# The output bias as a three-row product on PE, and the residual's product with the second gate on DVE, in a fused attention and expert layer

## The reference

```python
h = layernorm(x) * (1 + ca) + sa
x = x + ga * (attention(h) @ w_out + b_out)          # ga: the first gate, a row of 256 for each batch
h = layernorm(x) * (1 + cb) + sb
x = x + gb * experts(h)                              # gb: the second gate
```

## Time and profile before

| what | us |
|---|---|
| median of 3 timed runs | 1009.81 |
| span of the profiled execution | 1005.9 |
| PE busy in it | 722.7 (72%) |
| POOL busy | 653.6 (65%) |
| DVE busy | 543.6 (54%) |
| ACT busy | 376.4 (37%) |
| first stage, to the last exp | about 608 |
| from there to the first load of experts' rows | about 100 (608 to 708.3) |
| second stage | about 298 (708.3 to 1005.9) |

### The profile page before, as it was taken

The page is one execution under the profiler, slowest core; times in us unless marked ns, Lnnn a source line. Parts: engine busy times, 40 slices in busy tenths (PEclk is TensorE's granted clock), DMA queues, the critical chain, the costliest instruction groups (busy, mean ns, idle before and its releaser), DMA issues.

```text
span 1005.9 us, 15544 instructions
## 1 busy us (share of the span) xinstructions
PE 722.7 (72%) x4732; PEld 472.7 (47%) x4732; DVE 543.6 (54%) x1990; ACT 376.4 (37%) x827; POOL 653.6 (65%) x624
## 2 busy tenths in 40 slices
PE   4689998996987987987978774200699898888200
PEld 2345554553553553554554443200588776777100
DVE  3566588877877778786777673520122222222028
ACT  2145654553553553553533431100254333333100
POOL 5115340885885886885885556777388888888630
PEclk9789998996996997997996978555799999999655
DMA  8695976447446536524524558400699998898978
GB/s 301 182 345 171 357 252 222 138 158 229 160 144 228 171 127 207 180 102 156 165 94 143 169 155 253 132 8 4 202 257 283 259 251 160 154 164 173 227 210 327
DMA packets 165133, 191.58 MB, mean 190 GB/s; under 512 B 21497, under 2 KB 146581, under 8 KB 165052
## 3 DMA queue, kind: packets, MB, share of 16 engines
q1 hardware_dynamic: 128636, 134.27, 41.7%
q0 software_dynamic: 30720, 38.03, 18.6%
q10 hardware_dynamic: 5696, 18.30, 4.9%
HBM read 100.77 MB, written 110.67 MB: 210 GB/s over the span
## 4 chain that ended last, share of the span: by engine, by line
PE 32%; issue 18%; DVE 15%; DMA 14%; POOL 10%; SPq 4%; ACT 3%; another core or an unknown queue 3%; POOLq 0%; ACTq 0%; DVEq 0%
DMA acc_d<-ys,xg 8%; POOL acc_d L729 6%; PE stageA L957 4%; PE scores L985 4%; PE outT L1027 4%; DVE junk L1254 4%; PE scoresT L1007 3%; PE scoresT L1186 3%; SPq L355 3%; PE scoresT L1011 3%; DMA xt<-L_attn_x_dram 2%; PE stageA L967 2%; PE stageC L1064 2%; DVE pairs L1319 2%
## 5 line engine op out<-in xcount | busy, mean ns | idle before, releaser
L645 POOL DMA_INDIRECT slots_d<-H,dest x256 | 258.4, 1010 | 108.7 <-issue 62.7
L729 POOL DMA_INDIRECT acc_d<-ys,xg x128 | 198.2, 1548 | 61.0 <-issue 29.3
L1254 DVE CUSTOM_DVE_ANT_0 junk<-scores,mask 128x256 bf16<-128x256 f32 x512 | 187.9, 420 | 90.2 <-PE scores L985 63.7
L783 ACT ACTIVATE PT<-scoresT 128x512 f32<-128x512 f32 (+1 forms) x320 | 154.7, 508 | 151.5 <-PE scoresT L1011 104.4
L1186 PE MATMUL scoresT<-xgT,wgu 128*128 128x256 f32 x512 | 127.7, 393 | 23.6 <-ACT xgT L878 22.8
L985 PE MATMUL scores<-Ks,Qs 96*128 96x256 bf16 x512 | 108.8, 298 | 45.9 <-DVE mrowmax L1254 33.8
L1007 PE MATMUL scoresT<-mask,identb 128*128 128x512 bf16 (+1 forms) x320 | 117.6, 368 | 20.7 <-ACT PT L783 7.2
L1186 PEld LDWEIGHTS scoresT<-xgT,wgu 128*128 128x128 f32 x512 | 96.3, 194 | 48.4 <-ACT xgT L878 32.8
L1011 PE MATMUL scoresT<-Qs,Ks 98*128 98x256 bf16 (+1 forms) x640 | 118.1, 268 | 0.0
L1027 PE MATMUL outT<-PT,Va 128*32 128x256 f32 (+1 forms) x1280 | 95.0, 371 | 0.0
L598 POOL TENSOR_TENSOR r<-p,parts 128x512 f32<-128x512 f32 x32 | 39.2, 1224 | 77.8 <-ACT parts L775 76.3
(11 more groups left out here) (195 smaller groups left out, 1222.0 us busy)
## 6 DMA issues: line engine op xcount, KB each, us to landing
xg<-slots_d SPq DMA_DIRECT2D x64, 324.0 KB
slots_d<-blank ACTq DMA_DIRECT2D x26, 648.0 KB, 5.3
parts_d<-parts SPq DMA_DIRECT2D x32, 384.0 KB
Qs<-parts_d SPq DMA_DIRECT2D x96, 128.0 KB
Ks<-parts_d SPq DMA_DIRECT2D x90, 128.0 KB
acc_d<-zero SPq DMA_DIRECT2D x32, 272.0 KB
wgu<-L_ffn_w_gate_dram SPq DMA_DIRECT2D x64, 128.0 KB, 2.8
wgu<-L_ffn_w_up_dram SPq DMA_DIRECT2D x64, 128.0 KB, 2.9
```

The costliest lines, as they stand in the source:

```text
L645: pool.indirect_dma_start(out=slots_d[:, :], in_=H2[bt.par][:, t, :], in_offset=None, out_offset=bass.IndirectOffsetOnAxis(ap=dest[bt.par] ...
L729: pool.indirect_dma_start(out=acc_d[ACC[e]][:, :], in_=ys[e % NY][:, h, :], in_offset=None, out_offset=bass.IndirectOffsetOnAxis(ap=xg[e % ...
L783: sc_.activation(PT[m % NPT][:, :, 0:w], src, ACT.Exp).then_inc(sems["exp"], 1)
L1254: ins = v.tensor_tensor_reduce(out=junk[:, i, :], in0=bS[n % 2][:, i * 2 * P:(i + 1) * 2 * P], in1=mask[:, edge, :], scale=1.0, scalar=TAK ...
```

## The change

The bias goes to PE. Once, in the pass of batch 0 (slots 6 and 7), DVE splits b_out into three bf16 rows whose sum is b_out to 32 bits, and puts row 0 of the first part, row 1 of the second and row 2 of the third into one tile bo3, twice side by side (8 instructions, `out_bias`). In each `c_op` a bf16 product of three rows of ones with bo3, 512 columns wide, opens the bank, and the products with w_out are added to it. `c_xb` and its wait go; `c_x1` waits for the loads of xc and mr instead. `c_xs` moves from POOL to DVE, one slot earlier (10 for 11), and the store of x1 in SP's order one slot later (11 for 10). Behind the loop, `c_xs(last)` stands at the end of DVE's work for the last batch. The splits stay on POOL.

```diff
-    xb=(2,), onT=(2, 3), op=(4, 5), x1=(4, 5), x1_store=(10,), xs=(11,), ...
+    onT=(2, 3), op=(4, 5), x1=(4, 5), x1_store=(11,), xs=(10,), ...
 # POOL
-            def c_xb(bt):
-                after(pool, "c_ld", bt, 32)
-                after(pool, "xb", bt, 0)
-                gp.tensor_tensor(gbo[:], mr[:, 0, :], bo[:], ALU.mult).then_inc(sems["xb"], 1)
-                after(pool, "xb", bt, 1)
-                gp.tensor_tensor(xc[:], xc[:], gbo[:, :].unsqueeze(1).to_broadcast([P, T, D]), ALU.add
-                                 ).then_inc(sems["xb"], 1)
-            def c_xs(bt):
-                after(pool, "xn2", bt, T)
-                gp.tensor_tensor(x1[:], x1[:], mr[:, 3, :].unsqueeze(1).to_broadcast([P, T, D]), ALU.mult
-                                 ).then_inc(sems["xs"], 1)
...
             last = batch(B - 1)
             pre = batch(B - 2)
-            c_xb(last)
             for i in range(10):
                 send(pre, i)
             for half in range(2):
                 c_rstd(last, half)
-            c_xs(last)
 # PE, c_op
+                if bt.b == 0 and n == 0:
+                    pe.wait_ge(s_bo, 8)
+                mm(bank[:, :], onesb[0:3, :], bo3[0:3, :, :].rearrange("p i d -> p (i d)"), start=True, stop=False,
+                   skip_group_check=True)
...
-                                  start=(k == 0), stop=(k == C - 1))
+                                  start=False, stop=(k == C - 1), skip_group_check=True)
 # DVE
-                after(dve, "xb", bt, 2)
+                after(dve, "c_ld", bt, 32)
...
+            def c_xs(bt):
+                after(dve, "xn2", bt, T)
+                v.tensor_tensor(x1[:], x1[:], mr[:, 3, :].unsqueeze(1).to_broadcast([P, T, D]), ALU.mult
+                                ).then_inc(sems["xs"], 1)
+            def out_bias(part):
+                if part == 0:
+                    dve.wait_ge(s_par, 16 * 5)
+                    v.tensor_copy(selb[:], bo[:]).then_inc(s_bo, 1)
...
+                    for _ in at("xs", slot) if prev else []:
+                        c_xs(prev)
...
             e_key(last, LATE["cnt"])
+            c_xs(last)
```

More of the change, by code:

```diff
@@ L64 @@
     exp=10 * QUADS, pv=10 * QUADS, oTs=QUADS, oTp=QUADS, rec=QUADS, on=QUADS,
-    onTp=C, onT=C, op=2, t1=2, xb=2, x1=2, xs=1, stats2=T, aggr2=T, rstd2=8, xn2=T, h2=4, h2Tp=C, h2T=C,
+    onTp=C, onT=C, op=2, t1=2, x1=2, xs=1, stats2=T, aggr2=T, rstd2=8, xn2=T, h2=4, h2Tp=C, h2T=C,
     lg=1, ex=1, route=38, pre=T + 1, idc=1, cntp=1, key=2, near=T,
@@ L76 @@
     split=(-1, 0, 0, 1, 1, 2, 8, 8, 9, 9, 10, 10), store=(1, 3, 10, 11), stack=(4, 12), v=(9, 11, 13),
-    xb=(2,), onT=(2, 3), op=(4, 5), x1=(4, 5), x1_store=(10,), xs=(11,), stats2=(4, 5), c_rstd=(5, 6), xhat=(6, 7), norm2=(7, 8),
+    onT=(2, 3), op=(4, 5), x1=(4, 5), x1_store=(11,), xs=(10,), stats2=(4, 5), c_rstd=(5, 6), xhat=(6, 7), norm2=(7, 8),
     h2T=(9, 10), lg=(11,), route=(12, 13, 13, 14, 14, 15, 15, 16, 16, 17, 18, 18), cnt=(18,), key=(19,), zero=(3,),
@@ L191, in build @@
         s_fg = sem("gate_rows_loaded")
+        s_bo = sem("out_bias_steps")
         def sbt(stack, name, shape, dt=F32):
@@ L261, in build @@
         mr = sb("mr", [P, 4, D])
-        gbo = sb("gbo", [P, D])
+        bo3 = sb("bo3", [P, 2, D], BF16)
         x1 = sb("x1", [P, T, D])
@@ L663, in body @@
                         a_rstd(bt)
-                    for _ in at("xb", slot) if prev else []:
-                        c_xb(prev)
                     for half in at("c_rstd", slot) if prev else []:
@@ L671, in body @@
                         a_split(bt, n)
-                    for _ in at("xs", slot) if prev else []:
-                        c_xs(prev)
                     if now.b >= 2:
@@ L1310, in c_norm @@
                                     (ALU.mult, ALU.add)[k]).then_inc(sems["h2"], 1)
+            def c_xs(bt):
[6 more added lines that the diff above has]
+                    v.tensor_copy(selb[:], bo[:]).then_inc(s_bo, 1)
+                    dve.wait_ge(s_bo, 1)
+                    v.tensor_tensor(ex[:], bo[:], selb[:], ALU.subtract).then_inc(s_bo, 1)
+                    dve.wait_ge(s_bo, 2)
+                    v.tensor_copy(bo3[:, 1, :], ex[:]).then_inc(s_bo, 1)
+                    dve.wait_ge(s_bo, 3)
+                    v.tensor_tensor(sc[:], ex[:], bo3[:, 1, :], ALU.subtract).then_inc(s_bo, 1)
+                else:
+                    v.tensor_scalar(bo3[:, 0, :], selb[:], ident[:, 0:1], None, ALU.mult).then_inc(s_bo, 1)
+                    dve.wait_ge(s_bo, 5)
+                    v.scalar_tensor_tensor(bo3[:, 0, :], bo3[:, 1, :], ident[:, 1:2], bo3[:, 0, :], ALU.mult, ALU.add
+                                           ).then_inc(s_bo, 1)
+                    dve.wait_ge(s_bo, 6)
+                    v.scalar_tensor_tensor(bo3[:, 0, :], sc[:], ident[:, 2:3], bo3[:, 0, :], ALU.mult, ALU.add
+                                           ).then_inc(s_bo, 1)
+                    dve.wait_ge(s_bo, 7)
+                    v.tensor_copy(bo3[:, 1, :], bo3[:, 0, :]).then_inc(s_bo, 1)
             def c_route(bt, part):
@@ L1443, in body @@
                         mod_gates(slot - 1)
+                    if not prev and 6 <= slot <= 7:
+                        out_bias(slot - 6)
                     if u == 2 and ahead[0]:
```

## The result

The changed kernel took 998.11 us (median of four runs, 991.67 to 1004.87), the kernel before 1010.25 beside it (median of four, 1009.03 to 1015.16). The ratio is 0.9871, 95% interval 0.9826 to 0.9915. Forecast was 976; the time lies in the range of 960 to 1000. The profiled execution took 1000.8 us with a span of 999.1, so 6.8 us of span are to be explained, of 34.1 forecast. It is one execution, 2.7 us above the median. It also shows that start and end take 1.7 us outside the span, not the 3.9 assumed ahead of the prediction; that moves the forecast by 2 us and changes nothing else.

The account below looks back on a forecast made before the run. Passes are paced by short waits between PE, ACT and DVE; POOL alone sets the second stage's start. Terms -10.6-12.2-8-2.3-6+3.5+1+0.5 = -34.1 take the span from 1005.9 to 971.8, time 976 us (own range 966 to 986).

Parts of the forecast that it names:

- what slots 14 to 17 hold: Slots 14 to 17, batches 2 to 6: 106.0 us, 35.0 above batch 1, laid to held DVE steps, clock, sends, loads.
- the tail, -10.6: Behind the loop: POOL's sends no longer wait for the residual's sum and product, so the next send starts 10.6 us earlier.
- DVE held by POOL's product, -12.2: Slots 12 and 13: five long DVE steps held beside POOL's product return to normal, 12.2 us, all on the chain.
- what follows, -8: Slots 14 to 17: a third of the remaining 22.8 us (low clock, POOL's late sends, loads) comes back, 8 us.
- rival 2: Slots 14 to 17 fall to batch 1's length everywhere: -49, 961 us; chance 0.15.
- rival 1: Slots 14 to 17 stay long; only the tail, direct holds and slot 2 pay: -20, 990 us; chance 0.20.
- Slot 2, -2.3: Slot 2: without POOL's gbo step, DVE's second M step is no longer held, 0.47 us in five passes.
- transfers earlier, -6: Stores and loads from slot 2 come 3.1 us earlier, easing slot 8's M rows transfer: 1 us in six passes.
- PE's bias, +3.5: PE in the loop: 14 bias products of 0.22 to 0.43 us ahead of c_op's products add 3.5 us.
- DVE's product, +1: End of slot 10: DVE's product, 1225 ns in seven passes, mostly hidden, adds 1 us (0 to +16.8).
- Rival 4: Slower: DVE's product delays slot 11's maxima, PE's clock falls, bias costs 6: +24.5, 1034 us; chance 0.06.
- The steps that split the bias, +0.5, at most 2.5: Batch 0: the 8 small DVE steps, some 2.5 us in two slots, add 0.5 us, at most 2.5.

Follow-up runs that it names:

- the second chip: Changed kernel and kernel before rerun unchanged, on the second group's chip (979.3 us before): changed kernel 954.06 us, ratio 0.9741.
- the chip of the third group: Changed kernel rerun unchanged beside the kernel before, on a chip at 1009.6 us before: 1002.84 us, ratio 0.9929.
- the small product: Kernel before, with POOL's product of the residual with the second gate cut to 8 of 256 columns: 999.75 us, ratio 0.9904.
- seven sends first: Changed kernel with later bias rows; behind the loop seven sends, first half's norm steps, one send, second half's, instead of ten sends ahead: 993.42 us, 0.9834.

## Why the prediction was wrong

**The step that failed first: what slots 14 to 17 hold.** The prediction took the excess of slots 14 to 17 over batch 1, 35.0 us, as the price of VectorE's held steps, their clock and POOL's backlog, and gave 12.2 and 8 of it back. On the second chip, with product and sends where they were, the kernel before shows 84.7 us, and the change takes 5.3. The held steps were real there too (3.00, 3.16, 3.17, 2.80 and 1.63 us beside a product of 2.36) and the change removed them. Slot 15 of the five passes became 11.3 us shorter by it, but slots 14 and 17 grew by 2.8 and 3.3; what held them then has not been traced. The rest of the excess goes with the late updates: of unexplained waits the first profile had 126.8 us in ACT and DVE and the second 0.8. That sum overstates them, since all waits of the two engines between the first send and the load of rows are 376.5 us against 313.2, 63 more. The cue was in the page I read: waits "<-remote" on a single core, and long waits of ACT and DVE "<-issue".

**The step that cost most: the tail, -10.6.** On the first chip it came out at +1.6, and at +3.6 on the chip of the third group against the first chip's profile (98.1 to 99.7 and to 101.6). What failed there is "DVE did not wait for POOL's sum there but for PE, so this moment does not come earlier", read as if it would not come later either: the last step of the statistics starts 16.4 us behind the last exponential in the kernel before, and 26.5 and 26.4 in the two profiles of the changed one. Where updates come at once the tail gained 14.2, and the measured 88.1 us lies next to the 87.5 forecast. That is right as a mechanism, for POOL's sends then set the end alone, but the size is in part luck: there DVE did wait for POOL's sum, 10.29 us, and POOL 7.80 us for the gate rows instead of 3.01, and it is one profile of each kernel.

**Why later?** Six profiles are from chips with late updates. In the two whose POOL stands idle while the last inputs, gate rows and weights are loaded (the kernel before and its version with the small product), ACT's copy of the last outputs starts 3.4 and 1.3 us behind the last exponential, and the second copy of turned outputs at 7.5 and 5.9. In the four whose POOL sends all the time, 5.4, 8.3, 5.9 and 8.2, and 16.7, 16.5, 17.3 and 14.6. So the sends, which the change lets run at once, seem to be what makes updates late there, and to undo their own gain. The rest of the first stage speaks for it too: in all six profiles ACT and DVE together have at most 0.2 us of unexplained waits ahead of the first send (180 to 189 us), though 36 of the 96 loads of stacked queries are issued by then, and the first of PE's updates over 0.5 us late comes at 200 to 210 us. Against it: the second stage has another 128 indirect transfers from POOL and no update that late. These kernels differ in more than the sends, and the edits meant to isolate them met chips without the effect: it is likely, not shown.

**DVE held by POOL's product, -12.2, and what follows, -8.** Together 5.3 in slots 14 to 17 on the second chip and 8 on the first. Batches 2 to 6 gained 13.8 and 11.0 us in all; on the second chip the rest is in slots 4, 10, 11 and 19. On the second chip the stretch is nearly batch 1's (15.9 against 14.1 a pass), as rival 2 had it, but 21 of the 35 us it meant to win had never been the kernel's. On the first chip it stayed long, as rival 1 had it, and the tail's loss made it less than rival 1's 20 us.

**Slot 2, -2.3, and transfers earlier, -6.** Slot 2 itself did not move. Over five batches slot 4, where the attention output's first half is taken up, lost 3.4 us on the second chip and 1.7 on the first, slots 9 to 11 together 2.8 and 1.0, none of it forecast there; slot 8, where I expected the transfers to pay, did not move: 5.4 us before and after.

**PE's bias, +3.5.** Slots 5 and 6 grew by 1.5 and 1.6 us over five batches and slot 7 gave 1.6 back. The bias product has a mean of 384 ns:

```profile
L1043 PE MATMUL stageC<-bo,onesb 3*128 3x512 bf16 x14 | 5.4, 384 | 0.0
```

**DVE's product, +1.** Not contradicted: nothing measurable. It takes 1.2 to 1.8 us on the first chip, and on the second 2.8 in four of eight cases. The split that meets it takes 1.94 instead of 1.17. By the rule of the Trainium skill quoted in the prediction ("SBUF — State Buffer", "SBUF: two separate sides") each can hold the other, and these rows agree. Rival 4 needed this on the path and found it hidden.

**The steps that split the bias, +0.5, at most 2.5.** Wrong by some 3 us. Batch 0 takes 66.0, 63.8 and 63.3 us in the three profiles of the changed kernel, 60.8 to 66.1 in the nine other kernels with these steps in slots 6 and 7, 60.1 to 61.2 in the four with them in slots 15 and 16, where the eight take 2.91 us, and 58.0 to 59.7 in the four without them. Slot 9 shows the price without the scatter of the start: 6.9 to 8.7 us in the twelve profiles with them in slots 6 and 7, 4.2 in the eight others. I had counted their length and not that splits would hold two of them, or that the M step stands behind them. With the steps in slots 15 and 16, slot 19 is 0.8 us longer; what is left lies in slots 1 to 5, which take 16.1 to 20.8 us whatever the kernel.

In sum, for the two profiles of the first chip: +11.3 in the tail (to the load of rows, -10.6 against +0.7), +9.1 in the batches and +7.1 in batch 0 make 27.5 of the 27.3 us that the span missed.

## What to carry to other kernels

A wait that ends at nothing the profile shows need not be a property of the kernel: here the same programs had 127 us of them on one chip and 1 on another. Sum such waits before a stage's excess over another is laid to the change, and measure on a second chip. Moving work off an engine pays what that engine was last for, and a held step counts only as far as someone waits for its result. Put one-time set-up steps where nobody waits, and price them with what can hold them.

The lowest medians are those of the change with the bias rows built in slots 15 and 16: 952.1 and 952.0 us, 0.971 and 0.9723, where the change alone has 0.9741 (the intervals overlap). On the other kind these rows were tried only together with seven sends first: 0.9834, where the change alone has 0.9929.

## What the runs showed of the hardware

Semaphore updates can be recorded microseconds behind the instruction that makes them, on some chips and not on others, for the same program: 979 to 981 us on four chips, 1010 on two. Every chip was met in one session only, so the chip cannot be told from its circumstances. In the first profile of the changed kernel the last four updates of PE in the loop are recorded at 601.41, 602.83, 604.26 and 605.69 us, for products that ended by 600.8.

They are PE's. In the kernel before, up to 620 us, 57 of PE's 961 recorded updates lie over 1.5 us behind the last product that makes them, up to 7.80, and those of ACT, DVE and POOL all within 0.01. On the second chip none of PE's lies over 0.07 us behind. The traces of the first kind also lack records: 961 of PE's 1097 updates and 948 of DVE's 1219 are there, on the second chip 1091 of 1101 and 1219 of 1236. So some of the waits called "issue" were ended by an update in good time that left no record.

The DMA engines are not slower there. Windows from slots 16 and 17 of batch 3 in the kernel before, of the first chip and of the second:

```profile
312.00:316.00 4.00, 1.24 (x7) 0.43 (x7) 1.49 (x9) 1.36 (x3) 0.97 (x1) 0.92 0.90 288
```

```profile
307.00:311.00 4.00, 4.00 (x25) 2.33 (x24) 3.76 (x19) 1.37 (x3) 3.06 (x3) 0.56 0.93 306
```

The same share and rate of transfers (0.90 and 0.93 of their time, 288 and 306 GB/s), but PE has 1.24 us of work in the one and 4.00 in the other. What makes such a chip, and which transfers trigger it, stays open.
